# Attention block on one core: every score slot seeded by ScalarE, and the next batch's statistics and chunks re-timed

## The reference

```python
xn = (xg - mean) * jax.lax.rsqrt(var + EPS)              # per group of 16 channels
xn = xn.reshape(b, c, T) * gn_w[None, :, None] + gn_b[None, :, None]
qkv = jnp.einsum('oc,bct->bot', qkv_w, xn) + qkv_b[None, :, None]
q, k, v = jnp.split(qkv.reshape(b * N_HEADS, 3 * ch, T), 3, axis=1)
weight = jnp.einsum('bct,bcs->bts', q * scale, k * scale)
weight = jax.nn.softmax(weight, axis=-1)
a = jnp.einsum('bts,bcs->bct', weight, v).reshape(b, c, T)
hout = jnp.einsum('oc,bct->bot', proj_w, a) + proj_b[None, :, None]
return (xn + hout).reshape(b, c, h, w)
```

## Time and profile before

| what | us |
|---|---|
| median of 3 runs (lowest, highest) | 3937.64 (3936.87, 3939.83) |
| the profiled execution, its own time | 3937.71 |
| its span (first to last instruction) | 3936.0 |
| TensorE busy | 3842.4 (98%) |
| GpSimd busy | 3002.6 (76%) |
| ScalarE busy | 2275.7 (58%) |
| VectorE busy | 2223.0 (56%) |
| mean granted TensorE clock, share of full | 0.994 |

### The profile page before, as it was taken

One profiled execution on the slowest core, in us unless ns is written; L12 is line 12 of the kernel. 1 busy time (PEld: TensorE's weight loads), 2 busy tenths in 40 slices (PEclk: granted clock), 3 DMA queues, 4 the chain that ended last, 5 costly groups with the idle time before them and its releaser, 6 DMA issues.

```text
span 3936.0 us, 77117 instructions
## 1 busy us (share of the span) xinstructions
PE 3842.4 (98%) x31730; PEld 2451.3 (62%) x31730; DVE 2223.0 (56%) x2821; ACT 2275.7 (58%) x3173; POOL 3002.6 (76%) x1639
## 2 busy tenths in 40 slices
PE   6999999999999999999999999999999999999998
PEld 3566565656756566565675656666567565656656
DVE  4555555574555555556555555556655555555553
ACT  2665555565555555656556555555655555555664
POOL 0788888887488888877748888887774888888894
PEclk9999999999999999999999999999999999999999
DMA  2000000131400000012140000002214000000014
GB/s 77 15 20 25 16 22 21 40 90 43 137 20 18 23 22 19 22 52 82 35 141 19 22 21 17 25 18 75 62 44 130 22 18 22 20 19 19 19 35 133
DMA packets 133679, 165.18 MB, mean 42 GB/s; under 512 B 61648, under 2 KB 110800, under 8 KB 132816
## 3 DMA queue, kind: packets, MB, share of 16 engines
q1 hardware_dynamic: 133328, 160.26, 13.1%
HBM read 122.17 MB, written 38.04 MB: 41 GB/s over the span
## 4 chain that ended last, share of the span: by engine, by line
PE 66%; POOL 4%; DVE 2%; DMA 1%; issue 1%; ACT 0%; POOLq 0%; SPq 0%; DVEq 0%; ACTq 0%
PE oacc L606 20%; PE scores L586 16%; PE pool_bank L524 10%; PE aux_banks L546 8%; PE pool_bank L536 5%; POOL denom L1129 3%; PE scores L582 3%; PE scores L686 2%; PE pool_bank L563 1%; DMA out<-probs 1%; DVE maxima L904 1%; DMA probs<-x 0%; ACT probs L791 0%; DVE probs L1065 0%; DVE att_lo L1008 0%
## 5 line engine op out<-in xcount | busy, mean ns | idle before, releaser
L1129 POOL TENSOR_TENSOR denom<-denom,probs 128x768 f32<-128x768 f32 x1536 | 2826.5, 1840 | 529.6 <-ACT probs L791 347.0
L904 DVE TENSOR_REDUCE maxima<-aux_banks 128x2 f32<-128x640 f32 x1728 | 1657.9, 959 | 1318.3 <-PE aux_banks L546 1288.9
L791 ACT ACTIVATE probs<-scores 128x768 f32<-128x768 f32 x1728 | 1310.8, 810 | 1247.3 <-PE scores L586 1231.2
L606 PE MATMUL oacc<-probs,vals 128*64 128x384 f32 x6912 | 1280.4, 491 | 0.0
L606 PEld LDWEIGHTS oacc<-probs,vals 128*64 128x64 f32 x6912 | 478.6, 137 | 512.0 <-issue 394.7
L546 PE MATMUL aux_banks<-k_hi,q_hi 64*128 64x448 f32 (+1 forms) x3456 | 683.4, 391 | 41.2 <-DVE maxima L904 35.0
L804 ACT ACTIVATE scores<-seeds 128x768 f32<-128x768 f32 x864 | 703.0, 814 | 12.0 <-PE scores L593 9.8
L546 PEld LDWEIGHTS aux_banks<-k_hi,q_hi 64*128 64x128 f32 x3456 | 323.2, 184 | 584.4 <-issue 448.6
L586 PE MATMUL scores<-q_hi,k_hi 64*128 64x384 f32 x3456 | 586.7, 335 | 7.6 <-ACT scores L804 7.4
L586 PE MATMUL scores<-q_lo,k_hi 64*128 64x384 f32 x3456 | 588.0, 335 | 0.0
L586 PE MATMUL scores<-q_hi,k_lo 64*128 64x384 f32 x3456 | 584.8, 334 | 0.0
(11 more groups left out here) (94 smaller groups left out, 1673.4 us busy)
## 6 DMA issues: line engine op xcount, KB each, us to landing
seeds<-neg_rows SPq DMA_DIRECT2D x96, 384.0 KB, 3.5
xtile<-x SPq DMA_DIRECT2D x72, 384.0 KB, 3.2
att<-o_norm SPq DMA_DIRECT2D x96, 192.0 KB, 1.9
probs<-x SPq DMA_DIRECT2D x24, 768.0 KB, 5.1
out<-probs SPq DMA_DIRECT2D x24, 768.0 KB, 6.8
xtile<-att SPq DMA_DIRECT2D x12, 768.0 KB, 4.6
att_raw<-att SPq DMA_DIRECT2D x12, 768.0 KB, 7.3
neg_rows<-neg_cols SPq DMA_DIRECT2D x384, 0.8 KB
```

Source lines behind the costliest of these rows:

```text
L606: ins = mm(oacc[head(e), 0:N], vals[p % 2][:, kt, head(e)], prob(s)[:, e * N:(e + 1) * N], start=(kt == 0), stop=(kt == KT - 1))
L791: a(prob(s).rearrange("p (h n) -> p h n", n=N), scores[:, s % 2, :, 0:N], ACT.Exp, scale=SCALE).then_inc(probs_ready, 1)
L904: v.tensor_reduce(maxima[:, :, qt, kc], aux_banks[:, :, 0:UNIT_KEYS[kc % 2]], AX.X, ALU.max)\
L1129: gp.tensor_tensor(acc, acc, prob(s), ALU.add).then_inc(added, 1)
```

## The change

Five things are changed:

- All slots are seeded by ScalarE. `shares` and its two matmuls at odd steps go; ScalarE issues two seeds a slot, after the two exponentials. At the end of the projection it also seeds step 1 of the next batch. SyncE waits for 18 seeds of a block instead of 9 before the buffer is overwritten.
- Max units take 256 and 512 keys instead of 320 and 448.
- VectorE takes the low parts of q and k chunks one slot later: behind the reduction of the next slot's first unit, ahead of the reciprocal's piece and the statistics.
- The statistics of the next batch move one pair ahead, to the third pair: steps 44, 46, ... 66 (slots 22 to 33), mean in slot 38, variance in slot 47, coefficients in slot 49. The loads of x for them move along.
- In the last pair, own q chunks stand in halves in slots 0, 1, 3, 4, 5, 6, 7, 8; normalising in slots 9 to 20; the 14 chunks of the next batch in quarters and halves from slot 13 to slot 53. Slots 2, 9 to 12, 20, 29, 38 and 47 hold none.

```diff
-    UNIT_KEYS = (320, 448)
+    UNIT_KEYS = (256, 512)
...
-    LAST_OWN_Q = (0, 1, 3, 4)
-    LAST_NEXT_K = (21, 22, 25, 26, 28, 30)
-    LAST_NEXT_Q = (32, 34)
-    LAST_NEXT_V = (35, 36, 37, 39, 40, 41)
-    STATS_AT, STATS_EVERY = 1, 2
-    MEAN_SLOT, VAR_SLOT, COEF_SLOT = 13, 14, 15
-    NORM_AT, NORM_EVERY = 33, 2
+    LAST_OWN_Q = (((0, 0, 2), (1, 2, 4)), ((3, 0, 2), (4, 2, 4)), ((5, 0, 2), (6, 2, 4)), ((7, 0, 2), (8, 2, 4)))
+    LAST_RUNS = ((13, (1, 1, 2)), (16, (1, 1, 1, 1)),
+                 *((r + d, n) for r in (21, 30, 39) for d, n in ((0, (1, 1, 2)), (3, (1, 1, 2)), (6, (2, 2)))),
+                 *((r, (2, 2)) for r in (48, 50, 52)))
+    STATS_AT, STATS_EVERY = 44, 2
+    MEAN_SLOT, VAR_SLOT, COEF_SLOT = 38, 47, 49
+    NORM_AT, NORM_EVERY = 18, 2
+    COEF_AT = (PAIRS - 2) * SLOTS + COEF_SLOT
...
-        STATS_STEPS = {LAST_S0 + STATS_AT + STATS_EVERY * n: n for n in range(XITEMS)}
+        STATS_S0 = (PAIRS - 2) * STEPS
+        STATS_STEPS = {STATS_S0 + STATS_AT + STATS_EVERY * n: n for n in range(XITEMS)}
...
                 if n >= 2:
-                    sp.wait_ge(seeded, PRIMED + KT // 2 * (n - 1))
-                    sp.wait_ge(probs_ready, PROBS_PRIMED + KT * (n - 1))
+                    sp.wait_ge(seeded, PRIMED + KT * (n - 1))
...
                 slot = scores[:, s % 2, :, 0:N]
-                if s % 2 == 0:
-                    pe.wait_ge(seeded, PRIMED + BSTEPS // 2 * b + s // 2 + 1)
-                else:
-                    if s >= 2:
-                        pe.wait_ge(probs_ready, PROBS_PRIMED + BSTEPS * b + s - 1)
-                    if kt == 1:
-                        pe.wait_ge(seeds_in[blk % 2], 16 * (BLOCKS // 2 * b + blk // 2 + 1))
-                    for e in range(2):
-                        mm(slot[:, e, :], shares[head(e), :], seeds[blk % 2][head(e), e * N:(e + 1) * N],
-                           start=True, stop=False)
+                pe.wait_ge(seeded, PRIMED + BSTEPS * b + s + 1)
...
-                a(scores[:, 0, :, 0:N], seeds[blk % 2][:, :].bitcast(fp32).rearrange("p (e n) -> p e n", n=N),
+                a(scores[:, s % 2, :, 0:N], seeds[blk % 2][:, :].rearrange("p (e n) -> p e n", n=N),
                   ACT.Copy).then_inc(seeded, 1)
...
-                    if GS * i + 2 < BSTEPS:
-                        seed(GS * i + 2, b)
+                    for s in range(GS * i + 2, min(GS * i + 4, BSTEPS)):
+                        seed(s, b)
...
+                    if n == PJ - 1 and not last:
+                        seed(1, b + 1, PRIMED + PJ * b + n + 1)
...
+            def low_parts(items):
+                return [key for key in completed(items) if key[0] in "qk"]
+
             def stream(b, last):
                 before, _ = PLANS[last]
-                for i in range(PAIRS * SLOTS):
-                    for s in range(GS * i, GS * i + GS):
+                for i in range(PAIRS * SLOTS + 1):
+                    for s in range(GS * i, min(GS * i + GS, BSTEPS)):
                         unit_of_step(s, b, last)
+                        if s % GS == 0 and i:
+                            for key in low_parts(before[i - 1]):
+                                behind(key, b, last)
                         for blk, piece in PIECES_AT.get(s, ()):
                             take_recip(b, blk, use(b, last, ("finish", blk // CH, blk % CH)), piece)
                         if s in STATS_STEPS and not last:
                             take_stats(STATS_STEPS[s], b + 1)
...
-                    if i == (PAIRS - 1) * SLOTS + COEF_SLOT and not last:
+                    if i == COEF_AT and not last:
                         coefs(b + 1)
```

More of the change, by code:

```diff
@@ L90, in batch_plan @@
             else:
-                chunks = list(zip(own_q, LAST_OWN_Q))
+                for key, parts in zip(own_q, LAST_OWN_Q):
+                    for s, a, b in parts:
+                        before[s0 + s].append((key, a, b))
                 if more_batches:
[L93 to L97, removed]
+                    for key, (s, parts) in zip(next_k + next_q + next_v, LAST_RUNS):
+                        done = 0
+                        for n in parts:
+                            before[s0 + s].append((key, done, done + n))
+                            s, done = s + 1, done + n
+            if p == PAIRS - 2 and more_batches:
+                whole(before, s0 + MEAN_SLOT, ("groupmean", PAIRS, 0))
+                whole(before, s0 + VAR_SLOT, ("groupvar", PAIRS, 0))
             for j in range(CH):
@@ L180, in attention_block_program @@
         k_lo = [sb(f"k_lo{i}", [128, T], fp32r) for i in range(2)]
-        seeds = [sb(f"seeds{i}", [128, 2 * N], fp32r) for i in range(2)]
-        shares = sb("shares", [128, 128], fp32r)
+        seeds = [sb(f"seeds{i}", [128, 2 * N]) for i in range(2)]
         xn = sb("xn", [128, CT, T])
@@ L203, in attention_block_program @@
         maxima = sb("maxima", [128, 2, KT, CH])
-        neg_max = sb("neg_max", [128, 32], fp32r)
+        neg_max = sb("neg_max", [128, 32])
         neg_cols = sb("neg_cols", [128, 32])
@@ L381, in send_max @@
                 if n >= 2:
-                    sp.wait_ge(seeded, PRIMED + KT // 2 * (n - 1))
-                    sp.wait_ge(probs_ready, PROBS_PRIMED + KT * (n - 1))
-                sp.dma_start(seeds[par][:, :].bitcast(fp32), neg_rows.rearrange("r q -> (r q)").partition_broadcast(128))\
+                    sp.wait_ge(seeded, PRIMED + KT * (n - 1))
+                sp.dma_start(seeds[par][:, :], neg_rows.rearrange("r q -> (r q)").partition_broadcast(128))\
                   .then_inc(seeds_in[par], 16)
@@ L398, in stream @@
                     kind = kind_of(p)
-                    if s == LAST_S0 and not last:
+                    if s == STATS_S0 and not last:
                         sp.wait_ge(xn_ready, XITEMS * (b + 1))
@@ L586, in make_scores @@
                         last = mm(slot[:, e, :], ks[head(e), keys], qs[head(e), queries],
-                                  start=False, stop=(n == 2), skip_group_check=(s % 2 == 0))
+                                  start=False, stop=(n == 2), skip_group_check=True)
                 last.then_inc(scores_full, 1)
             def open_banks():
-                for e in range(2):
-                    last = mm(scores[:, 0, e, 0:N], k_hi[0][head(e), 0:128], q_hi[head(e), chunk(0)],
-                              start=True, stop=True)
+                for slot in range(2):
+                    for e in range(2):
+                        last = mm(scores[:, slot, e, 0:N], k_hi[0][head(e), 0:128], q_hi[head(e), chunk(0)],
+                                  start=True, stop=True)
                 last.then_inc(banks_opened, 1)
@@ L692, in _ @@
             pe.sem_inc(pv_done, PRIMED)
-            pe.wait_ge(consts_made, 5)
+            pe.wait_ge(consts_made, 4)
             units = 0
@@ L881, in batch @@
                 projection(b, last)
-            act.wait_ge(consts_made, 5)
-            seed(0, 0, PRIMED)
+            act.wait_ge(consts_made, 4)
+            for s in range(2):
+                seed(s, 0, PRIMED)
             for b in range(B):
@@ L1043, in stream @@
                             take_stats(STATS_STEPS[s], b + 1)
-                    for key in completed(before[i]):
-                        behind(key, b, last)
-                    if i == (PAIRS - 1) * SLOTS + COEF_SLOT and not last:
+                    if i == PAIRS * SLOTS:
+                        for key in low_parts(before[i - 1]):
+                            behind(key, b, last)
+                    else:
+                        for key in completed(before[i]):
+                            if key[0] not in "qk":
+                                behind(key, b, last)
+                    if i == COEF_AT and not last:
                         coefs(b + 1)
```

5 lines of the change are left out of this document (2 added, 3 removed).

## The result

The changed kernel takes 3851.22 us (median of 4 runs, 3850.95 to 3852.81) against 3937.8 for the kernel before: 86.6 us less, a ratio of 0.978 with a 95% interval of 0.9768 to 0.9791. The direction was forecast and the size was not: 38 us were predicted. The time lies in the range (3825 to 3949), near rival A (3839).

A forecast was written before the change was run, and what follows sets the result against it. TensorE, busy 98% of the span, was taken to bound the kernel. Inner pairs -26, third pairs +38, last pairs -49.5, batch 3's last pair -1 and edges +0.5 sum to -38 us: 3899.5 us, range 3825 to 3949.

The forecast's parts named there:

- rival A: Low parts and o_norm: the new waits don't appear, VectorE starting sooner than added up; 3839 us, chance 0.26.
- The slot: Each TensorE-bound slot: seed removal and shorter first reduction make it 0.135 us shorter, bounds 0.03 and 0.173.
- It waits 0.06: Second max unit: its weight load can come 1.18 us after the first unit, TensorE arrives at 1.11.
- The low parts: Where a q or k chunk follows another at once: TensorE waits 0.17 us for pool_bank, 8 times a pair, 1.4 us.
- o_norm: Slot 4 of a block: o_norm waits for a GpSimd add, costing 0.5 us a block, 3.0 a pair; bounds 0.1, 1.15.
- The third pair: Third pairs of three batches: statistics cost 15.5 us, less 2.9 gained, so 12.6 slower each; bounds 9 and 22.
- The last pair: Last pairs of three batches: 222.9 against 239.4 us, 16.5 gained each, 49.5 in all; bounds 10 and 22.
- Batch edges: Behind the projection: the extra seed costs 0.1 to 0.2 us each, 0.5 in all.
- Batch 3's end: Batch 3's last pair: bound by GpSimd's adds, it gains only its first block's 1.0 us.
- B: Slot 4 of each block: o_norm waits behind a whole GpSimd add, 1.15 instead of 0.5 us; 3952 us, chance 0.08.
- C: Last pair gains nothing: ScalarE's 5 operations a slot delay slots up to 20 and chunks that follow; 3949 us, chance 0.07.
- D: Slots don't shorten: the first reduction takes 0.8 us with 256 keys too, only 0.03 gained a slot; 3981 us, chance 0.05.

The follow-up runs named there:

- the first experiment: The changed kernel with max units of 320 and 448 keys again, nothing else: 3932.73 us, ratio to the kernel before 0.999.
- the experiment that takes it away: The changed kernel with a chunk's first piece behind the probs x values products wherever the slot before completed a q or k chunk: 3830.19 us.
- short adds: The changed kernel with GpSimd's adds cut to 8 of 768 columns, save each block's first (output not the reference's): 3791.3 us.
- the fourth experiment: The changed kernel with statistics, normalising and the last pair's whole chunks placed as in the kernel before; seeds, key counts, low parts as changed: 3869.19 us.

## Why the prediction was wrong in size, point by point

The prediction's waits are nearly all where it put them; what failed is the size of three terms of its sum, all too dear. They make up the 48.5 us between -38 and -86.5: 23 in the inner pairs (12 the slot, 11 `o_norm`), 23 in the third pairs (15 the statistics, the rest slot and `o_norm`), 4 in the last pairs, less 2 at the edges and the end. The time lies in the range only because the range's lower end was set by rival A.

**The slot** (0.135 forecast, 0.16 measured, 774 slots: some 19 us). The failed step is "It waits 0.06": the second unit's weights do load when I said (1.18 us behind the first unit's), but that wait costs nothing, because a load up to 0.25 behind the one before it is still in time (the first experiment), and this one is at 0.25. The second unit's matmul comes 0.17 behind the last scores matmul, as if nothing had waited. I then charged the second unit's 64 more columns (0.03), and the 64 fewer of the first were lost in the wait. The gate at 320 keys is real: 0.13 a slot. "Already level" was the right reading of the rows before but for 0.04; that is why taking the seed off alone gains so little.

**The low parts** (0.17 a place forecast): 0.18 to 0.19 measured, and 21 us in all by the experiment that takes it away. Right.

**o_norm** (0.5 a block forecast, 0.30 measured: 0.2 in 72 inner blocks, 14 us). The mechanism was right: a GpSimd add holds it, by the 0.548 us that it takes without one and by its end 0.41 behind the add's. The size failed in "no slack is left": from the product's row to the next reduction's there was a gap of 0.10, and a row of VectorE may begin 0.08 before the last one ends (1319.01 + 1.66 = 1320.67, the next at 1320.59), so 0.18 was left. The product now ends 0.31 later after its slot's start and the reduction's data come 0.19 sooner; 0.31 + 0.19 - 0.18 = 0.32 is how late the reduction begins (1320.59, where 0.43 behind the unit would be 1320.27), and the slot is 0.30 longer. The Trainium skill (SBUF — State Buffer, "Who interferes with whom") has the rule that a VectorE operation with two SBUF inputs contends with a GpSimd operation that reads SBUF. The traces agree: 0.548 for all 96 with short adds, 1.64 in the median beside long ones. The coefficients' TENSOR_SCALAR (L970) has one tensor input and took 1.72 too, and 0.17 with short adds. The same section of the Trainium skill names this kind among the operations that can enter a two-port mode and then contend.

**The third pair** (15.5 of extra work forecast, 10.6 measured: 230.0 less 219.4). Nearly all of it, 9.9, is slots 49 and 50, where I had 10.5 for the square root and the coefficients. The failed step is the count of waits before that, 5.1: slots 18 to 44, with all statistics and the mean, are together 0.4 longer than in the third pair without them (the fourth experiment), and slot 47, with the variance, 0.3. VectorE's timeline in slot 30 after, which begins at 1605.24, shows the error:

```profile
1605.67 0.69 DVE L905 TENSOR_REDUCE maxima<-aux_banks 128x2 f32<-128x512 f32 x1 [0.49 <-PE aux_banks L553]
1606.28 0.57 DVE L987 STREAM_TRANSPOSE turned<-pool_bank 128x384 f32<-128x384 f32 x1
1606.78 0.98 DVE L934 BATCH_NORM_STATS2 stats<-xtile 128x6 f32<-128x384 f32 x2
1607.80 0.31 DVE L939 BATCH_NORM_AGGREGATE meanvar<-stats 128x2 f32<-128x36 f32 x1
1607.82 0.06 DVE L938 MEMSET spare<- 128x1 f32 x1
1608.02 1.16 DVE L905 TENSOR_REDUCE maxima<-aux_banks 128x2 f32<-128x1024 f32 x1
```

Each operation begins 0.05 to 0.1 before the row of the last one ends (0.69 long, 0.61 to the next; 0.57 and 0.50). "I count 0.65 ... 0.75 ... 0.8" added durations with gaps between, five operations to a slot: half a microsecond too much, where the slack was as small. And the small waits that statistics bring (0.07 in slot 29, 0.16 in 30, 0.18 in 33) are partly paid back by `o_norm`, which comes later against the adds: it takes 0.75 us in slot 31 (1612.79), and slot 32 reads 4.40 in place of 4.65.

**The last pair** (16.5 forecast, 17.9 measured, a third of 53.7). Right within 1.4. ScalarE is all but full in slots 9 to 20, as forecast: it is busy 45.8 of 46.8 us there (47.3 forecast). Slots 17 to 19 are nevertheless at TensorE's own 3.69.

```profile
1751.50:1798.30 46.80, 45.31 (x332) 24.62 (x330) 28.16 (x33) 45.77 (x63) 39.24 (x22) 1.00 0.34 95
```

**Batch edges** (0.5 forecast, 3.3 measured): a term I left out. The last slot holds half a v chunk now, and the projection's first matmul comes 3.10 us after the last exponential where it came 1.93 after it. With the old placing it is 1.96 again. It is the other side of the spread.

**Batch 3's end** (-1 forecast, -2.1 measured): 1.1 is the first block's shorter slots. The other 1 is what two large changes leave: the fourth block is 3.9 shorter (its `finish` waits 1.1 for GpSimd's add, and slots 29 and 30 read 5.18 and 3.05 where they read 7.00 and 4.79), and the fifth is 2.6 longer, since in its first slot ScalarE waits 2.83 for the DMA of the seeds (1.65 before), so slot 36 reads 7.46 for 4.94. The prediction called this pair GpSimd's throughout; the second of these waits is not GpSimd's.

**The rivals.** A in its strict form (no new waits) is false: the low parts' and `o_norm`'s are there, and only that of the units is not. It was near in time only since each of my waits was too dear. B, C and D are out: 0.30 and not 1.15 in slot 5, 17.9 us in the last pair, 0.69 us for the first reduction.

## What to carry to other kernels

When two engines arrive at a hand-over at the same time, shortening one gains little, and the edit that unlocks it (here 64 keys moved from one unit to the other) can look worthless too where the other engine is the later one: try both together. A sum over small waits should be made from start-to-start distances and not from durations with gaps, and a wait earlier in the pattern is to be taken off the waits behind it. Once the cause of a wait is known, the cheap cure is often to move it into a slot with room, or put other work before it, without making anything shorter: that brought 69 us here.

## What the runs showed of the hardware that was not expected

- Rows of VectorE overlap: the next operation begins 0.05 to 0.1 us before the row of the last one ends, and ScalarE's by 0.1 (two exponentials of 0.81 are 1.51).
- A weight load held back to 0.25 us behind the load before it (0.17 without a wait) cost nothing: the matmul behind it began at its usual 0.17 distance. Held back to 0.38 it cost 0.14, and to 0.55 it cost 0.30; some 0.10 of either came behind the held pair of matmuls.
- A VectorE operation on 4 values a partition lasted up to 1.79 us beside GpSimd's adds and 0.15 to 0.18 with short ones; `o_norm` 0.548 and up to 2.18. A held `o_norm` ended 0.41 to 0.42 after the add that held it.
